# Probabilities normalised on VectorE and ScalarE instead of GpSimd, and a new opening on TensorE

## The reference, cut to what matters

```python
# block 1: group norm (32 groups of 4 channels), attention over all 256 tokens, residual
xg = (xg - mean) / jnp.sqrt(var + EPS)                    # EPS = 1e-5
h = xg * scale + bias
q, k, v = h @ wq + bq, h @ wk + bk, h @ wv + bv
attn = softmax(q @ k.T * c ** -0.5, axis=-1)              # 256 x 256 per image
x = (attn @ v) @ wo + bo + x
# block 2: linear attention, 8 heads of 16 channels
q, k, v = heads of (x @ w_qkv + b_qkv)
q = softmax(q, axis=-1)                                   # over the 16 channels of a head
k = softmax(k, axis=-2)                                   # over the 256 tokens
context = einsum('nelk,neld->nekd', k, v)
out = einsum('nekd,nelk->neld', context, q) @ w_out + b_out
y = x + out * sigmoid(gamma) + beta
```

## Time and profile before

| | |
|---|---|
| median of 3 runs | 70.1 us (69.97 to 70.32) |
| the profiled execution | 70.25 us |
| its span, first to last instruction | 68.4 us |
| busy share of the span | PE 86%, PEld 79%, POOL 72%, DVE 61%, ACT 61% |
| mean granted TensorE clock | 0.975 |

### The profile page before, as it was taken

How to read it: one execution, slowest core, us unless ns; L and a number is a source line. 1 busy time by engine, 2 the same in 40 slices (tenths; PEclk the granted TensorE clock), 3 DMA queues, 4 the chain that set the end, 5 groups by cost and what they waited for, 6 DMA issues and landing times.

```text
span 68.4 us, 1147 instructions
## 1 busy us (share of the span) xinstructions
PE 59.1 (86%) x373; PEld 54.1 (79%) x373; DVE 41.9 (61%) x135; ACT 41.6 (61%) x133; POOL 49.0 (72%) x78
## 2 busy tenths in 40 slices
PE   2999999999968998897599999999999519899930
PEld 2898989879958787895599979999999317899810
DVE  2166957227998865489084868463878064984570
ACT  0722207417994998986299988778484093756600
POOL 4872910592899599999959899725999999873000
PEclk9999999999999999999999999999999995599999
DMA  0889500000000000000000000000000202002244
GB/s 0 227 193 327 214 0 0 0 0 0 0 10 5 0 5 0 0 0 5 0 0 0 0 10 0 0 0 0 0 0 0 77 0 77 0 10 77 77 156 150
DMA packets 2886, 2.77 MB, mean 40 GB/s; under 512 B 448, under 2 KB 2752, under 8 KB 2880
## 3 DMA queue, kind: packets, MB, share of 16 engines
q1 hardware_dynamic: 2448, 2.43, 11.5%
q10 hardware_dynamic: 432, 0.27, 1.3%
HBM read 1.64 MB, written 1.05 MB: 39 GB/s over the span
## 4 chain that ended last, share of the span: by engine, by line
PE 44%; POOL 33%; DVE 8%; DMA 6%; ACT 2%; issue 1%; SPq 1%
POOL probs L257 14%; POOL y_all L265 11%; PE bank L1054 6%; DMA xT_all<-in_x 6%; PE bank L1039 4%; PE bank L1048 4%; PE bank L1079 3%; PE bank L1033 3%; PE bank L1074 3%; PE bank L1084 3%; PE bank L1087 3%; POOL q L268 3%; PE bank L1029 3%; POOL hT_lo L252 2%; POOL x1T_lo L261 2%; DVE y_all L727 2%
## 5 line engine op out<-in xcount | busy, mean ns | idle before, releaser
L257 POOL TENSOR_SCALAR probs<-probs,s_inv 128x256 f32<-128x256 f32 x14 | 13.0, 945 | 1.9 <-DVE s_inv L694 1.8
L415 ACT ACTIVATE probs<-bank,neg_smax 128x256 f32<-128x256 f32 x16 | 7.5, 479 | 2.0 <-DVE neg_smax L691 2.0
L1054 PE MATMUL bank<-probsT,vals 128*128 128x256 f32 x32 | 8.1, 379 | 0.0
L1079 PE MATMUL bank<-k_exp,v 128*128 128x128 f32 x32 | 5.8, 320 | 2.3 <-ACT v L430 2.3
L691 DVE TENSOR_REDUCE neg_smax<-bank 128x2 f32<-128x512 f32 x8 | 5.5, 688 | 3.0 <-PE bank L1039 1.9
L265 POOL TENSOR_SCALAR y_all<-x1T,y_bias 128x256 f32<-128x256 f32 x8 | 7.3, 924 | 0.1
L1079 PEld LDWEIGHTS bank<-k_exp,v 128*128 128x128 f32 x32 | 5.3, 232 | 2.6 <-ACT v L430 2.5
L261 POOL TENSOR_TENSOR x1T_lo<-x1T,x1T_hi 128x256 fp32r<-128x256 f32 x8 | 5.8, 731 | 1.7 <-ACT x1T_hi L423 1.7
L1048 PE MATMUL bank<-ident,probs 128*128 128x128 f32 x32 | 5.0, 280 | 2.1 <-POOL probs L257 2.0
L420 ACT ACTIVATE probsT<-bank 128x512 f32<-128x512 f32 x8 | 4.8, 602 | 3.0 <-PE bank L1048 2.9
L433 ACT ACTIVATE q<-q 128x256 f32<-128x256 f32 x8 | 3.3, 428 | 4.9 <-POOL q L268 4.9
(11 more groups left out here) (116 smaller groups left out, 188.0 us busy)
## 6 DMA issues: line engine op xcount, KB each, us to landing
xT_all<-in_x SPq DMA_DIRECT2D x8, 128.0 KB, 3.9
out_y<-y_all SPq DMA_DIRECT2D x8, 128.0 KB, 1.7
one_s<-in_w_one SPq DMA_DIRECT2D x1, 320.0 KB, 4.1
qk_s<-in_w_qk ACTq DMA_DIRECT2D x1, 128.0 KB, 2.8
vo_s<-in_w_vo ACTq DMA_DIRECT2D x1, 128.0 KB, 4.1
vec<-in_vectors ACTq DMA_DIRECT2D x1, 5.0 KB, 3.0
```

The source lines that it names most:

```text
L257: p = pool.tensor_scalar(probs[:, b, j, :], probs[:, b, j, :], s_inv[:, b, j:j + 1], None, ALU.mult)
L415: e = act.activation(probs[:, b, j, :], full(S_PS[b])[:, j, :], ACT.Exp, bias=neg_smax[:, b, j:j + 1], accum_out=s_sum[:, b, j:j + 1])
L1054: m = pe.matmul(wide(ATT_PS[b]), vals[:, b, k, :], probsT[:, b, k, :], start=(k == 0), stop=(k == J - 1))
L1079: m = pe.matmul(square(CTX_PS[b]), v1[:, b, j, :], k_exp[:, b, j * C:(j + 1) * C], start=(j == 0), stop=(j == J - 1))
```

## The change

- POOL's `normal_probs` goes. DVE takes images 0, 1, 3 and 2 (one 128x512 instruction each), ACT takes images 5, 4, 6 and 7 (two 128x256 instructions each, a Copy with a scale per partition).
- EPS is no longer added by products: `gather_eps` and the two memsets of `added_eps` go, and DVE gets `add_eps`, a tiny addition after each of the five `group_stats`.
- PE's opening: 11 unread products in place of 9, then `a_product`, the gathers of images 0 and 1 with nothing else around them, and 6 more unread products.
- `x1_plus_bias` on POOL is a TENSOR_TENSOR with the bias broadcast along the row, where it was a TENSOR_SCALAR; it now runs as soon as `x1_sum` is done, and `y_bias_product`, `add_beta` come early.
- The queues of all engines are written in a new order (images in the order 0, 1, 3, 2, 5, 4, 6, 7; image 1 is stored last) and the bank tables are new. `vec` gets an eleventh column that no step reads. v's copy has a new name.

```diff
-        A_PS, AB_PS, WVO_PS, VB_PS, YB_PS = 3, 2, 5, 5, 1
+        A_PS, AB_PS, WVO_PS, VB_PS, YB_PS = 0, 3, 4, 0, 2
...
-            def normal_probs(b):
-                for j in range(J):
-                    p = pool.tensor_scalar(probs[:, b, j, :], probs[:, b, j, :], s_inv[:, b, j:j + 1], None, ALU.mult)
-                p.then_inc(pn_pool, 1)
...
-                pool.tensor_scalar(y_all[:, b, :], x1T[:, b, :], y_bias[:, :], None, ALU.add).then_inc(x1b_ready, 1)
+                pool.tensor_tensor(y_all[:, b, :], x1T[:, b, :], y_bias[:, :].to_broadcast([P, L]), ALU.add).then_inc(x1b_ready, 1)
...
+            def normal_probs(b):
+                for j in range(J):
+                    p = act.activation(probs[:, b, j, :], probs[:, b, j, :], ACT.Copy, scale=s_inv[:, b, j:j + 1])
+                p.then_inc(pn_act, 1)
...
+            def add_eps(n):
+                a, z = STAT_SETS[n]
+                dve.tensor_scalar(mv[:, a:z, 1], mv[:, a:z, 1], EPS, None, ALU.add).then_inc(veps_ready, 1)
...
             pe.wait_ge(rest_set, 1)
-            turn_over(9)
-            pe.wait_ge(eps_ready, 1)
-            gather_eps(1)
+            turn_over(11)
+            pe.wait_ge(qk_in, 16)
+            a_product()
...
+            turn_over(6)
```

More of the change, by code:

```diff
@@ L326, in _ @@
             pool.wait_ge(qmax_ready, 1)
-            q_shift(1)
-            pool.wait_ge(qmax_ready, 2)
             q_shift(0)
[L330 to L333, removed]
+            pool.wait_ge(x1T_ready, 4)
+            x1_plus_bias(5)
+            pool.wait_ge(x1T_ready, 5)
+            x1_plus_bias(4)
             pool.wait_ge(x1T_hi_ready, 4)
-            x1T_low(4)
-            pool.wait_ge(qmax_ready, 3)
@@ L349, in _ @@
             x1T_low(7)
+            pool.wait_ge(x1T_ready, 8)
+            x1_plus_bias(6)
+            pool.wait_ge(qinv_ready, 5)
+            q_normal(4)
             pool.wait_ge(x1T_hi_ready, 8)
[L351 to L369, removed]
-            q_shift(5)
-            pool.wait_ge(qinv_ready, 5)
+            x1T_low(6)
+            q_normal(1)
+            pool.wait_ge(qinv_ready, 6)
             q_normal(2)
             pool.wait_ge(qmax_ready, 7)
-            q_shift(4)
+            q_shift(7)
@@ L567, in _ @@
             act.wait_ge(m_done, 1)
             m_copy(0)
+            val_copy(7)
+            act.wait_ge(kmax_ready, 4)
+            k_exp_t(5)
+            act.wait_ge(qb_ready, 2)
+            v_half_copy(5)
+            k_copy(3)
+            act.wait_ge(smax_ready, 8)
+            s_exp(7)
+            act.wait_ge(qsh_ready, 2)
+            q_exp(5)
+            act.wait_ge(kmax_ready, 5)
+            k_exp_t(4)
+            act.wait_ge(s_inv_ready, 8)
+            normal_probs(7)
+            v_half_copy(4)
@@ L787, in _ @@
+            add_eps(4)
+            dve.wait_ge(scales_ready, 4)
+            h_norm(5)
+            dve.wait_ge(probs_ready, 1)
+            s_recip(0)
+            h_norm(4)
+            dve.wait_ge(s_inv_ready, 1)
+            normal_probs(0)
+            dve.wait_ge(rstd_ready, 5)
+            set_scales(4)
             dve.wait_ge(s_done, 2)
             s_max(1)
-            dve.wait_ge(gather_done, 5)
-            group_stats(4)
-            dve.wait_ge(probs_ready, 1)
-            s_recip(0)
@@ L806, in _ @@
[L806 to L808 removed]
+            dve.wait_ge(s_inv_ready, 2)
+            normal_probs(1)
             dve.wait_ge(s_done, 3)
             s_max(3)
[L811 to L814 removed]
+            dve.wait_ge(u_hi_ready, 3)
+            u_low(5)
+            u_low(2)
+            dve.wait_ge(u_hi_ready, 4)
+            u_low(4)
+            dve.wait_ge(att_done, 1)
@@ L872, in _ @@
[L872 to L887 removed]
+            q_maxima(0)
```

1066 lines of the change are left out of this document (531 added, 535 removed).

## The result

The changed kernel takes 62.34 us (median of 4 runs, 61.66 to 62.58) against 70.21 for the kernel before on the same chip: a ratio of 0.887, 95% interval 0.878 to 0.897. The forecast was 63.6 us with a range of 61.5 to 67.9. The profiled execution took 61.66 us, with a span of 59.9 and 1.76 outside it. A ratio compares, of each kernel, only the runs within about 1.5% of its fastest one; beside it, or without one, stands the range of all runs.

The account below looks back on a forecast made before the run. PE, the fullest engine at 86%, bounds the kernel, idling on POOL's queue. 16.5 opening + 38.5 products + 1.9 small steps + 2.1 added waits + 2.7 tail + 1.85 outside the span gives 63.6 us; range 61.5 to 67.9.

Parts of the forecast that it names:

- The sum: Whole kernel: p_transposes(0) at 16.5, plus products 38.5, small steps 1.9, added waits 2.1, tail 2.7, outside 1.85: 63.6 us.
- I take it that the clock now rises in the opening: Opening: wide PE work raises the clock, DVE's 9.2 us queue then sets p_transposes(0) at 16.5 for 18.22; chance 0.50.
- Rival 1: Opening: the clock does not rise, PE sets it, p_transposes(0) comes at 18.7, time 65.8 us; chance 0.25.
- A third of it reaches PE, 2.1 us: After p_transposes(0): of 6.4 us added to ACT and DVE, a third delays PE, 2.1 us; bounds nothing and 6.4.
- the 1.9 of small steps kept: From p_transposes(0) to the last product: PE's 1.9 us lost in small steps behind waits stays as before.
- My own bound "nothing": Lower bound for added ACT and DVE work reaching PE: none, as PE covers waits with other images' products.
- Rival 2: ACT and DVE queues: in order, so all 6.4 us added reach PE instead of 2.1; 67.9 us, chance 0.12.
- So 8.3 us are lost: PE from p_transposes(0) to the last product, before: 5.1 us idle, 1.3 by low clock, 1.9 in small steps.
- The prices: Busy times expected: POOL 49.0 to 33.6 us, ACT 41.6 to 45.2, DVE 41.9 to 44.7; x1_plus_bias 924 to 621 ns.
- rival 3: SBUF port: POOL instructions block DVE's normalising three times at 0.7 us, adding 2.1 us; 65.7 us, chance 0.05.
- Rival 4: Middle: new queues make two or more PE idle stretches with the low clock behind; 70.8 or 74.4 us, chance 0.08.
- The signs: Trace marks for right or wrong: u_plain(0) at 0.43 or 1.06 us, PE waits, DVE normalising over 1 us, mid-kernel clock.

Follow-up runs that it names:

- The double dose: The changed kernel with each of ACT's eight normalising instructions preceded by an unread copy of the same product, 3.2 us more in all: 62.31 to 65.81 us.

## Why the prediction was right, and where it was not

**The sum.** By the profiled execution it comes out as 17.72 + 38.5 (products) + 0.9 (all losses; the last product ends at 57.11) + 2.8 (tail) + 1.76 = 61.7 us, against 16.5 + 38.5 + 1.9 + 2.1 + 2.7 + 1.85 = 63.6. The 38.5 is the prediction's own estimate; of the 0.9 only 0.25 is idle time of PE. Tail and the time outside the span were right to 0.1 us. Two steps were off, with opposite signs: the opening by 1.2 us too early, the losses by 3.1 too large. That the sum misses by 1.9 us and not by 3.1 is luck, as is which opening the profiled execution had: with the early rise the same kernel took 58.89, below the range.

**"I take it that the clock now rises in the opening": wrong for the profile on which the result is read, and ill-posed.** `u_plain(0)` took 1.06. The 17 unread products do not bring the rise by themselves; in the changed kernel it came at 5 us in one profile and at 13.6 in the other. Neither gives the 16.5. With the early rise `p_transposes(0)` comes at 14.59, below even the lower bound of 15.6. DVE then goes from `h_norm(0)` at 6.54 to the end of `normal_probs(0)` at 14.40, 7.9 us for the 9.2 of the sum: its instructions overlap. And `h_norm(0)` came 0.7 us earlier than the forecast 7.3 also in the first profile (6.63), as DVE's `group_stats(0)` no longer stands behind `channel_stats(2)`, which had waited for its image's transfer; `a_low` ahead of `set_rstd(0)` cost 0.1 us. Rival 1's premise thus held in the result's profile, but its 18.7 was too late by 1.0: it had `u_plain(1)` and what follows at the slow pace, while the pace rose at 13.6. (With the rise near 16 us, two profiles have 18.74 and 18.85.)

**"A third of it reaches PE, 2.1 us": mis-sized, as was the 1.9 of small steps kept.** Together 0.9 us were lost. So the added work cost at most that, and at least half of the old small steps behind waits went too. The double dose shows why a fixed share was the wrong form: here the cost is next to nothing until ACT is full, and then everything. My own bound "nothing" was the right end. The 83% that I had for ACT was an average over three stages; in the first it became 97% (14.87 of 15.30 us), which the average hid. Rival 2 (the loss comes back) is wrong for this change, but right for the same move in the old order: there ACT and the late queue took all of it back.

**"So 8.3 us are lost", and what takes them away: the account held, its attribution did not.** Of the 8.3, 0.9 are left. But I gave the 2.5 us of idle PE in 18.2 to 33.3 to POOL's probabilities and the 2.6 and 1.3 of the later stretch to the five `x1_plus_bias`, as if each could be taken out by itself. The second holds for the most part: TENSOR_TENSOR alone took out 3.1 of the 3.9. The first doesn't: moved alone 0.3, moved with the other 0.2 more. The remaining 4.8 us came only with the new order and the moved probabilities together; as tried here, either without the other gave nothing of them (44.7 with both parts in the old order, 44.7 with the new order and POOL's probabilities, 44.9 with TENSOR_TENSOR alone; another place for POOL's probabilities would have kept up to 1.1). Which piece of the new order matters (the images' order, the early `x1_plus_bias`, the places in ACT's queue) was not taken apart and stays open. So does the 1.3 us for the low clock: three runs of the kernel before, at a mean granted clock of 1.00, took 69.41 to 69.92 us, and twelve at 0.975 took 69.57 to 70.79, median 70.0. Across an opening that varies, the 1.3 does not show there.

**The prices** were near. POOL 34.3 us for 33.6; `x1_plus_bias` 670 ns for 621, as it now meets DVE's instructions in rows like the one at 23.40 (in the old place it took 620); DVE 45.3 for 44.7. ACT came to 42.6 for 45.2: its normalising Copy reads 545 ns for my 450, but in a row four take 1.71 us from start to end, 0.4 each, as they overlap. The eight are busy for 3.7 us together; that ACT's total grew by 1.0 only I put down to its other steps overlapping more in the fuller queue, which no run isolates.

**The port, rival 3**, showed in the rows at 22.94 (0.37 us for DVE) and cost PE no idle time: none stands in its timeline before 30.5 us. Which engine waits depends on who is second, which I had not allowed for. The Trainium skill (SBUF — State Buffer, Who interferes with whom) says just this, that whoever starts second waits for all of the first; these rows agree to within 0.15 us.

**Rival 4** did not come: no idle stretch above 0.25 us on PE behind `p_transposes(0)`, and the clock at 1.00. What it says of the clock was seen from the other side: with the idle stretch at 0.33 us, in the old order too, the low clock behind it is gone.

**The signs.** Of those named for "wrong", two came: 1.06 us for `u_plain(0)`, and one of DVE's four normalising instructions at 1.06. The waits, the clock in the middle and POOL's busy time came as named for "right".

## What to carry to other kernels

An idle stretch that a chain charges to one engine need not be won by relieving that engine alone: where several queues are in order, the relief is worth what the next queue lets through, so test the part by itself before giving it a price. Give added work on an engine no fixed share: compare its busy time with the bottleneck's stage by stage, free while there is slack and in full when there is none. And look for a cheap form of an operation that stands in a row ahead of something on the path; here five instructions shorter by 0.3 us each took 3 us out of the body.

## What was not expected of the hardware

- The moment at which TensorE's pace rises in the opening differs between executions of the same program: 5 us in one profile of the changed kernel, 13.6 in another, up to 16 in kernels with the same opening. It moves `p_transposes(0)` by 3.1 us and the span by 2.8 (57.1 for 59.9). The granted-clock column reads 1.00 all the while. What decides the moment was not found; the wide unread products before it, 11 and 6, were the same in both.
- POOL takes 924 to 983 ns for a TENSOR_SCALAR with a scalar per partition and 613 to 670 for a TENSOR_TENSOR of the same size with the same column broadcast.
